# Scattering second choices between the experts' first tiles: a metaformer block with a top-2 mixture of experts on one core

## The chip, the cores and the metric

The kernel runs on one core of a Trainium2 chip. The metric is the device time of one execution in microseconds (us); lower is better. The engines are TensorE (PE), VectorE (DVE), ScalarE (ACT), GpSimd (POOL) and SyncE (SP), which here only issues DMAs and waits. "Line" and L followed by a number mean a line of the kernel before.

## What is computed

The input x is 128 images x 256 channels x 9 x 9 pixels, float32. A first part normalises each pixel over its channels, computes an attention-like convolution block and adds it to x. The second part, in which the change lies, is a mixture of experts over the 128 x 81 = 10368 tokens t (one token is one pixel of one image, 256 channels):

```
logits = layernorm(t) @ Wr.T + br                 # 8 experts
p      = softmax(logits); p1,e1,p2,e2 = top 2 of p
y      = p1 * ffn[e1](layernorm(t)) + p2 * ffn[e2](layernorm(t))
ffn[e](v) = gelu(v @ W1[e] + b1[e]) @ W2[e] + b2[e]   # 256 -> 512 -> 256
out    = t + y
```

Each token so goes to two experts, its first and its second choice; there are 20736 (token, expert) rows in all.

## The kernel before

**Stages.** Until about 733 us the first part runs, and leaves the tokens in SBUF. Then come three stages: routing (733 to 980 us), the experts' tiles (985 to 1510 us), and the sum of both results with the store of the output (to 1600 us).

**Routing** goes over the 81 pixels q in eight batches (6, six times 12, 3). Per batch PE turns the pixels (L637), ACT copies them out of PSUM (`turned`, L1382), DVE takes statistics (`pixel_parts`, L1045), computes probabilities and both choices (`choices`, L1087) and then the position of every row in its expert's region in DRAM (`positions`, L1115), with the help of two small PE products (`places`, L662). Position means: `base_s` (the expert's next free row) plus the number of earlier rows of that expert; first and second choices are counted together. ACT then builds one row block per pixel (`row`, L1407): 128 tokens x 260 numbers (256 channels, 4 tags) in `xf_s`, a ring of 18 slots. POOL scatters each block twice with an indirect DMA (L1546 to L1551), once to the first and once to the second choices' positions in `rows_d`: 162 scatters of 130 KB. A slot of the ring is taken again when both its scatters have landed (`landed`, L262; wait at L1413).

Beside this, SP loads the experts' weights in 32 pieces of 256 KB through three buffers (L378 to L381); ACT makes the high half (`high_piece`, L1418) and DVE the low half (`low_piece`, L1036) of each. Four pieces go with each batch; their places in the order of ACT and DVE are written out by hand (L1430 to L1448 and L1137 to L1146).

**Between routing and experts.** DVE gives the ends of the regions (`ends_c`, L1152), and SP writes 256 empty rows behind each expert's last row (L384 to L390). DVE computes the table `tabi_s` of 88 tiles (L1155 to L1180): for each tile of 256 rows its expert and its first row; then `base_c`. SP waits for the padding, all scatters, the table and the weights (L391 to L395), and starts the loads of rows. DVE waits for all scatters too, and then releases PE and ACT with `tab_r` (L1186).

**The experts' tiles.** There are always 88 tiles. For tile t: SP loads 256 rows (`load_rows`, L398), PE transposes them (`turn_rows`, L678), ACT and DVE split them into two float16 halves (L1454, L1188), PE multiplies (`up`, L689), ACT applies gelu, DVE splits again (L1218), PE multiplies (`down`, L707), DVE adds the bias (`scaled_rows`, L1225), ACT weighs the rows (`weighed`, L1470), POOL returns them with two indirect DMAs to `y_d` (`return_rows`, L1553). PE's order is transposes of t+1, up of t, down of t-1 (L728 to L733). ACT's order is `high_rows(t+1)`, `weighed(t-2)`, `gelu(t)` (L1482 to L1487). DVE ends an iteration with `scaled_rows(t-1)` and then `tags(t+1)`, which copies the tags out of the loaded rows and so frees their buffer. SP's turn t waits for the transposes and the tags of tile t and then loads tile t+2 into the same of two buffers:

```
with sp.Fori(1, TILES // 2 - 1) as i:
    for par in range(2):
        t = i * 2 + par
        sp.wait_ge(S["tt_p"], t + 1)
        sp.sem_inc(S["settle_s"], 1)
        sp.wait_ge(S["tag_c"], t + 1 + CREDIT)
        load_rows(t + 2, par)
```

`scaled_rows(t)` waits until the returns of tile t-2 have landed (L1228), as `yo_s` has two buffers.

## Time and profile before

| | us |
|---|---|
| median of 3 runs (lowest, highest) | 1610.61 (1609.75, 1611.9) |
| the profiled execution's own time | 1601.33 |
| its span, first to last instruction | 1599.6 |
| PE busy, share of the span | 1297.4, 81% |
| DVE busy | 1080.9, 68% |
| ACT busy | 771.0, 48% |
| POOL busy | 568.3, 36% |
| 162 scatters on POOL, L1549 | 158.6 busy |
| 176 returns on POOL, L1558 | 173.5 busy |

The profile comes from one execution, which took 9.3 us less than the median of the runs. Its page gives busy times over the whole span, so an engine with a small share can still be the last one in a stage. Other views give the same trace by stretches of time, by line of the kernel, or as the chain of work that ended last.

### The profile page before, as it was taken

The page shows a single profiled execution, that of the slowest core. Times are in us where ns is not written, and L with a number is a line of the kernel's source. Part 1 is how long each engine was busy: PE and PEld are TensorE (multiplying, and loading weights), DVE is VectorE, ACT ScalarE, POOL GpSimd, SP SyncE. Part 2 cuts the span into 40 slices and gives each one's busy share as a digit, 9 for nine tenths or more (in the row PEclk, how much of TensorE's full clock was granted, in tenths as well). Part 3 has the DMA queues.
Part 4 walks back from the last instruction along what each step waited for, and adds up shares of the span by engine and source line. Part 5 has one row for each costly group of instructions (what it writes and reads, how often), then busy time and mean ns, then how long its engine had stood idle before and what let it go on. Part 6 is the DMA issues. An engine that isn't in the chain of part 4 may idle for free.

```text
span 1599.6 us, 36879 instructions
## 1 busy us (share of the span) xinstructions
PE 1297.4 (81%) x9796; PEld 1072.9 (67%) x9797; DVE 1080.9 (68%) x2553; ACT 771.0 (48%) x1828; POOL 568.3 (36%) x561
## 2 busy tenths in 40 slices
PE   0197999999999999977656403999999999999592
PEld 0196999857676666657556302888888888888441
DVE  6797555378878788884656662777777777777462
ACT  0295666455444544442677761544555555555200
POOL 0163111333444334430577773333333333333200
PEclk9998999999999999985555555999999999999897
DMA  8635783858877978741243453222222222222297
GB/s 325 143 89 225 304 320 135 246 140 187 190 183 179 209 175 192 178 105 47 82 151 130 150 192 114 89 83 87 92 93 93 85 90 93 89 87 77 99 424 310
DMA packets 256214, 251.16 MB, mean 157 GB/s; under 512 B 149753, under 2 KB 234190, under 8 KB 251876
## 3 DMA queue, kind: packets, MB, share of 16 engines
q1 hardware_dynamic: 235789, 197.20, 41.1%
q0 software_dynamic: 20320, 53.45, 9.7%
q8 instruction: 18, 0.29, 0.1%
q14 instruction: 21, 0.17, 0.0%
q10 hardware_dynamic: 66, 0.05, 0.0%
HBM read 152.34 MB, written 105.75 MB: 161 GB/s over the span
## 4 chain that ended last, share of the span: by engine, by line
PE 56%; DVE 16%; DMA 10%; issue 6%; ACT 4%; SPq 3%; POOL 2%; DVEq 1%; ACTq 0%; POOLq 0%
PE ps L716 15%; PE ps L701 14%; PE ps L520 5%; PE ps L500 4%; PE ps L539 3%; DMA u_d<-in_zstrings 3%; PE ps L685 2%; DMA pool_<-k_d 2%; DMA pool_<-y_d 2%; POOL rows_d L1549 2%; PE ps L566 2%; SPq L291 2%; DMA pool_<-in_ffn_w 2%; PE ps L489 2%; ACT aux L1414 2%
## 5 line engine op out<-in xcount | busy, mean ns | idle before, releaser
L1558 POOL DMA_INDIRECT y_d<-pool_,to_s x176 | 173.5, 986 | 357.3 <-ACT pool_ L1473 328.0
L716 PE MATMUL ps<-pool_,aux 128*128 x2112 | 246.9, 273 | 4.9 <-DVE aux L1223 3.2
L701 PE MATMUL ps<-aux,pool_ 128*128 128x256 f16 x2112 | 247.1, 274 | 0.8 <-ACT aux L1466 0.6
L716 PEld LDWEIGHTS ps<-pool_,aux 128*128 128x128 f16 x2112 | 199.0, 98 | 47.4 <-issue 23.6
L701 PEld LDWEIGHTS ps<-aux,pool_ 128*128 x2112 | 207.2, 98 | 25.6 <-issue 1.4
L1549 POOL DMA_INDIRECT rows_d<-aux,idx_s x162 | 158.6, 979 | 105.7 <-ACT aux L1416 60.8
L1466 ACT ACTIVATE aux<-ps,b_s 128x256 f32<-128x256 f32 x352 | 138.1, 474 | 92.6 <-DVE aux L1223 92.5
L1458 ACT ACTIVATE aux<-ps 128x512 f16<-128x512 f32 x88 | 52.5, 597 | 187.0 <-PE ps L685 187.0
L1543 POOL DMA_DIRECT2D pool_<-v_d x64 | 50.0, 781 | 214.6 <-PE ps L599 213.2
L1231 DVE SCALAR_TENSOR_TENSOR pool_<-ps,pool_ 128x512 f32<-128x512 f32 x88 | 60.8, 691 | 92.4 <-PE ps L716 92.4
L539 PE MATMUL ps<-pool_,se_w_s 81*81 81x512 f32 x256 | 115.5, 593 | 3.6 <-DMA pool_<-k_d 3.6
L1223 DVE TENSOR_TENSOR aux<-aux 128x1024 f16<-128x1024 f32 x88 | 107.8, 1225 | 3.1
L1371 ACT ACTIVATE pool_<-ps,pool_ 128x81 f32<-128x81 f32 x256 | 79.5, 336 | 52.1 <-DVE pool_ L932 52.1
L883 DVE COPY aux<-ps 81x512 f32<-81x512 f32 x64 | 44.0, 687 | 71.5 <-PE ps L500 71.4
L685 PE MATMUL ps<-ident_s,pool_ 128*128 128x128 f32 x352 | 53.9, 276 | 44.1 <-DMA pool_<-rows_d 44.1
L520 PE MATMUL ps<-pool_,aux 82*128 82x162 f32 x512 | 85.6, 309 | 0.0
L1050 DVE BATCH_NORM_STATS2 aux<-big 128x6 f32<-128x256 f32 x81 | 45.0, 603 | 58.7 <-ACT big L1385 58.7
L665 PE MATMUL ps<-aux,before_s 128*128 128x8 f32 x16 | 4.8, 371 | 97.2 <-DVE aux L1112 97.2
L1473 ACT ACTIVATE pool_<-pool_,wrow_s 128x256 f32<-128x256 f32 x176 | 78.9, 498 | 9.1 <-DVE pool_ L1231 9.1
L1359 ACT ACTIVATE pool_<-ps,sa_ab 128x324 f32<-128x324 f32 x64 | 39.7, 620 | 86.6 <-PE ps L551 86.6
L1525 POOL COPY aux<-big 128x324 f32 x64 | 29.2, 457 | 138.6 <-PE ps L500 129.0
L1190 DVE TENSOR_TENSOR aux<-ps,aux 128x512 f16<-128x512 f32 x88 | 60.1, 683 | 24.8 <-ACT aux L1458 24.8
(204 smaller groups left out, 2974.4 us busy)
## 6 DMA issues: line engine op xcount, KB each, us to landing
pool_<-rows_d SPq DMA_DIRECT2D x88, 260.0 KB
pool_<-y_d SPq DMA_DIRECT2D x18, 1152.0 KB, 12.9
big<-in_x SPq DMA_DIRECT2D x2, 5184.0 KB, 21.2
xn_d<-big SPq DMA_DIRECT2D x8, 1296.0 KB, 4.8
v_d<-aux SPq DMA_DIRECT2D x64, 162.0 KB, 2.5
ks_d<-aux SPq DMA_DIRECT2D x64, 162.0 KB, 3.1
pool_<-xn_d SPq DMA_DIRECT2D x32, 324.0 KB
pool_<-k_d SPq DMA_DIRECT2D x32, 324.0 KB
```

The costliest lines, as they stand in the source:

```text
L500: last = nc.tensor.matmul(ps[0:HW, 4 + par, c * BS:(c + 1) * BS], xq_s[:, par, c, :], ident_s[:, :], start=True, stop=True)
L520: last = nc.tensor.matmul(o, pt_s[:, par, c, :], m_s[:, side, k * QUAD + c, :, :] .rearrange("p v n -> p (v n)"), start=True, stop=True)
L539: last = nc.tensor.matmul(ps[0:HW, n, :], se_w1_s[:, k, :], kq_s[:, par, k, 2 * n:2 * n + 2, :].rearrange("p b j -> p (b j)"), start=k == ...
L685: last = nc.tensor.transpose(ps[:, par, h * SLOTS + s * 128:h * SLOTS + (s + 1) * 128], rin_s[:, par, s, h * 128:(h + 1) * 128], ident_s[: ...
L701: last = nc.tensor.matmul(o, w_s[:, a, bass.ds(e * (4 * PIECE) + (k * HID + j * 128), 128)], xh_s[:, par, b, k * SLOTS:(k + 1) * SLOTS], s ...
L716: last = nc.tensor.matmul(ps[:, 6 + par, s * C:(s + 1) * C], hh_s[:, par, a, j, s * 128:(s + 1) * 128], w_s[:, b, bass.ds(e * (4 * PIECE) ...
L1223: nc.vector.tensor_tensor(lo, hf_s, hi, ALU.subtract).then_inc(S["hlo_c"], 1)
L1371: ins = nc.scalar.activation(e_s[:, par, h, b, :], ps[:, 2 + h, b * HW:(b + 1) * HW], ACT.Exp, bias=sm_s[:, par, 2, j:j + 1], accum_out=sm ...
L1466: nc.scalar.activation(hf_s[:, j * SLOTS:(j + 1) * SLOTS], ps[:, 2 + 2 * par + j // 2, (j % 2) * SLOTS:(j % 2 + 1) * SLOTS], ACT.Gelu, bia ...
L1473: ins = nc.scalar.activation(yo_s[:, par, s, :], yo_s[:, par, s, :], ACT.Copy, scale=wrow_s[:, par, s:s + 1])
L1549: nc.gpsimd.indirect_dma_start(out=rows_d[:, :], out_offset=bass.IndirectOffsetOnAxis(ap=idx_s[:, k, q:q + 1], axis=0), in_=xf_s[:, q % RI ...
L1558: nc.gpsimd.indirect_dma_start(out=y_d[:, :], out_offset=bass.IndirectOffsetOnAxis(ap=to_s[:, par, k:k + 1], axis=0), in_=yo_s[:, par, k, ...
```

## The change

First choices and second choices get separate counts, so that in each expert's region all first choices stand ahead of all second choices. During routing POOL scatters only first choices. SP stores the row blocks, three pixels at a time, plainly in a new DRAM tensor `xrow_d`. `SURE` = 33 is the number of tiles that hold only first choices whatever the routing (full tiles: at least (10368 - 8 x 255) / 256); the table of tiles now gives these full tiles of all experts first, then the rest, with 16 entries in place of 8. After the table DVE computes the second choices' positions (`idx2f_c`). SP loads the stored blocks back, three pixels (`THIRD`) at a time in 27 batches b, through two buffers `late_s`, and POOL scatters them in between the returns: 6 ahead of the first return, then 75 spread over 29 tiles (`late_before`). In SP's order a batch is loaded in turn `late_turn(b)`, behind the load of rows of that turn, after a wait for all scatters of batch b-2.

```diff
+THIRD = 3
+LATE = HW // THIRD
+SURE = -(-(BS * HW - EXPERTS * (SLOTS - 1)) // SLOTS)
+        xrow_d = dram("xrow_d", [HW, 128, WIDE])
+        def late_before(t):
+            return min(HW, 2 * THIRD + (HW - 2 * THIRD) * t // (SURE - 4))
+        def late_turn(b):
+            return 1 + min(t for t in range(SURE) if late_before(t) >= (b - 1) * THIRD)
...
-            for n in range(PIECES):
+            def load_piece(n):
                 if n >= 3:
                     sp.wait_ge(S["wlo_c"], n - 2)
                 sp.dma_start(stage_s[:, n % 3], ffn_w[n]).then_inc(S[f"wst_in{n % 3}"], 16)
+            def keep_rows(q):
+                sp.wait_ge(S["xft_c"], q + THIRD)
+                slot = q % RING
+                sp.dma_start(xrow_d[q:q + THIRD].rearrange("q b c -> b q c"),
+                             xf_s[:, slot:slot + THIRD, :]).then_inc(S[f"rst{slot // THIRD}"], 16)
+            for j in range(len(BATCHES)):
+                for n in range(4 * j, 4 * j + 3):
+                    load_piece(n)
+                for q in range(FIRST[j], FIRST[j + 1] - THIRD, THIRD):
+                    keep_rows(q)
+                load_piece(4 * j + 3)
+                keep_rows(FIRST[j + 1] - THIRD)
...
+            def load_late(b):
+                if b >= 2:
+                    sp.wait_ge(S[f"late_out{b % 2}"], b // 2 * (16 * THIRD))
+                sp.dma_start(late_s[:, b % 2], xrow_d[b * THIRD:(b + 1) * THIRD].rearrange("q b c -> b q c")
+                             ).then_inc(S[f"late_in{b % 2}"], 16)
+            def next_rows(t, par):
+                sp.wait_ge(S["tt_p"], t + 1)
+                sp.sem_inc(S["settle_s"], 1)
+                sp.wait_ge(S["tag_c"], t + 1 + CREDIT)
+                load_rows(t + 2, par)
             load_rows(0, 0)
             load_rows(1, 1)
+            sp.wait_ge(S["idx2f_c"], 1)
+            for b in range(2):
+                load_late(b)
+            for t in range(SURE - 2):
+                next_rows(t, t % 2)
+                for b in range(2, LATE):
+                    if late_turn(b) == t:
+                        load_late(b)
+            for k in range(2):
+                sp.wait_ge(S[f"late_out{k}"], 16 * THIRD * len(range(k, LATE, 2)))
+            for t in range(SURE - 2, SURE - 2 + SURE % 2):
+                next_rows(t, t % 2)
...
@@ choices, positions (DVE); places (PE) takes 16 columns
-                link(nc.vector.tensor_tensor(hot_s[:, 2, 0:n, :], hot_s[:, 0, 0:n, :], hot_s[:, 1, 0:n, :], ALU.add))
-                nc.vector.reduce_sum(tot_s[:, :], hot_s[:, 2, 0:n, :].rearrange("p s e -> p e s"),
+                nc.vector.reduce_sum(tot_s[:, :, :], hot_s[:, :, 0:n, :].rearrange("p k s e -> p k e s"),
-                    link(nc.vector.tensor_tensor(at_s[:, s + 1, :], at_s[:, s, :], hot_s[:, 2, s, :], ALU.add))
+                    link(nc.vector.tensor_tensor(at_s[:, s + 1], at_s[:, s], hot_s[:, :, s, :], ALU.add))
-                nc.vector.tensor_copy(idx_s[:, 1, lo:hi], top_s[:, 0, 0:n]).then_inc(S["idx_c"], 1)
...
@@ the table (DVE)
-            for e in range(1, EXPERTS):
+            for e in range(1, 2 * EXPERTS):
                 link(nc.vector.tensor_tensor(ends[:, e:e + 1], ends[:, e:e + 1], ends[:, e - 1:e], ALU.add))
-            full = [1, TILES, EXPERTS]
+            full = [1, TILES, 2 * EXPERTS]
...
+            link(nc.vector.tensor_copy(starts[:, full_ones], firsts[:, full_ones]))
+            link(nc.vector.tensor_tensor(starts[:, 1:EXPERTS], firsts[:, 1:EXPERTS], firsts[:, one_less], ALU.subtract))
+            link(nc.vector.tensor_tensor(spread_s, pos2_s[:, :].unsqueeze(2).to_broadcast(wide),
+                                         region_s[:, :].unsqueeze(1).to_broadcast(wide), ALU.is_ge))
+            link(nc.vector.tensor_tensor(spread_s, spread_s, starts[:, full_ones].unsqueeze(1).to_broadcast(wide), ALU.mult))
+            link(nc.vector.reduce_sum(moved, spread_s, axis=AX.X))
+            link(nc.vector.tensor_tensor(moved, moved, pos2_s[:, :], ALU.add))
+            nc.vector.tensor_copy(idx_s[:, 1, :], moved).then_inc(S["idx2f_c"], 1)
             for k in range(RING):
                 dve.wait_ge(S[f"scat{k}"], landed(HW - RING + (k - HW) % RING))
+            for g in range(RING // THIRD):
+                dve.wait_ge(S[f"rst{g}"], kept(g))
...
                     act.wait_ge(S[f"scat{slot}"], landed(q - RING))
+                    act.wait_ge(S[f"rst{slot // THIRD}"], 16 * (q // RING))
...
@@ POOL
-                for k in range(2):
-                    nc.gpsimd.indirect_dma_start(
-                        out=rows_d[:, :], out_offset=bass.IndirectOffsetOnAxis(ap=idx_s[:, k, q:q + 1], axis=0),
-                        in_=xf_s[:, q % RING, :], in_offset=None).then_inc(S[f"scat{q % RING}"], 16)
+                nc.gpsimd.indirect_dma_start(
+                    out=rows_d[:, :], out_offset=bass.IndirectOffsetOnAxis(ap=idx_s[:, 0, q:q + 1], axis=0),
+                    in_=xf_s[:, q % RING, :], in_offset=None).then_inc(S[f"scat{q % RING}"], 16)
...
-            with pool.Fori(0, TILES // 2) as i:
+            pool.wait_ge(S["idx2f_c"], 1)
+            sent = 0
+            for t in range(SURE - SURE % 2):
+                for q in range(sent, late_before(t)):
+                    b = q // THIRD
+                    pool.wait_ge(S[f"late_in{b % 2}"], 16 * (b // 2 + 1))
+                    nc.gpsimd.indirect_dma_start(
+                        out=rows_d[:, :], out_offset=bass.IndirectOffsetOnAxis(ap=idx_s[:, 1, q:q + 1], axis=0),
+                        in_=late_s[:, b % 2, q % THIRD, :], in_offset=None).then_inc(S[f"late_out{b % 2}"], 16)
+                sent = late_before(t)
+                return_rows(t, t % 2)
+            with pool.Fori(SURE // 2, TILES // 2) as i:
                 for par in range(2):
                     return_rows(i * 2 + par, par)
```

## Rows read from the trace of the kernel before

**Rows 1.** Busy time of each engine in two stretches: window, us, engines, PEclk, DMA share, GB/s

```profile
955.00:985.00 30.00, 0.00 (x0) 0.00 (x0) 7.55 (x25) 0.00 (x0) 19.33 (x20) 0.50 0.51 174
...
1005.00:1200.00 195.00, 194.26 (x1743) 168.82 (x1741) 141.92 (x336) 98.60 (x234) 65.38 (x67) 1.00 0.27 89
```

**Rows 2.** Chain that ended last, 980 to 990 us: start, us, what

```profile
979.16 2.43 DMA rows_d<-aux,idx_s
...
981.65 0.03 SPq L393
...
981.72 0.03 SPq L393
...
982.14 0.28 SPq L399
...
982.88 0.42 SPq L400
...
984.06 2.93 DMA pool_<-rows_d
...
987.03 1.11 PE ps L685 x4
```

**Rows 3.** Line L685, the transposes of a tile: duration ns, first and last start

```profile
L685 PE MATMUL ps<-ident_s,pool_ x352: 272/273/474, 985.5 to 1489.0; 128*128 128x128 f32 x176
```

**Rows 4.** Line L1549, the scatters: duration ns min/median/max, and landing

```profile
L1549 POOL DMA_INDIRECT rows_d<-aux,idx_s x162: 956/960/1365, 759.8 to 979.2; - x162
...
DMA to landing us min/median/max: 2.4/2.4/4.6
```

**Rows 5.** Chain that ended last, routing, around one load of weights

```profile
892.91 3.58 DMA pool_<-in_ffn_w
...
897.15 0.98 ACT big L1385
```

**Rows 6.** Timeline from 950 to 963 us: start, us, engine, line, operation

```profile
950.84 0.19 ACT L1416 ACTIVATE aux<-ptag_s 128x4 f32<-128x4 f32 x1
...
952.91 9.28 SPq L387 DMA_DIRECT2D rows_d<-aux  x8
...
956.74 1.39 DVE L1164 TENSOR_TENSOR til_s<-til_s 128x1 f32<-128x1 f32 x7
...
958.16 0.88 DVE L1168 TENSOR_TENSOR aux<-til_s,turn_s 1x704 f32<-1x704 f32 x1
...
963.08 0.19 DVE L1180 CAST tabi_s<-aux 1x88 int32<-1x88 f32 x1
```

**Rows 7.** Timeline of one tile in the steady stretch, all engines

```profile
1052.38 0.60 PE L685 MATMUL ps<-ident_s,pool_ 128*128 128x128 f32 x4
...
1053.32 0.16 DVE L1196 COPY tag_s<-pool_ 128x8 f32<-128x8 f32 x1
...
1053.60 0.90 ACT L1473 ACTIVATE pool_<-pool_,wrow_s 128x256 f32<-128x256 f32 x2
...
1054.30 12.18 SPq L400 DMA_DIRECT2D pool_<-rows_d  x3
...
1055.37 0.98 POOL L1558 DMA_INDIRECT y_d<-pool_,to_s  x1 [3.48 <-ACT pool_ L1473]
...
1056.66 0.98 POOL L1558 DMA_INDIRECT y_d<-pool_,to_s  x1 [0.30 <-issue]
```

**Rows 8.** Line L381, the issues of weight loads on SP's queue

```profile
L381 SPq DMA_DIRECT2D pool_<-in_ffn_w x32: 340/341/1079, 733.9 to 951.0; - x32
```

**Rows 9.** Chain that ended last, an early and a late tile's transposes

```profile
1000.25 0.44 PE ps L685 x4
...
1488.81 0.44 PE ps L685 x4
```

**Rows 10.** Lines L1221 and L1042 on VectorE: duration ns min/median/max

```profile
L1221 DVE CAST aux<-aux x88: 682/685/693, 994.2 to 1501.1; 128x1024 f16<-128x1024 f32 x88
...
L1042 DVE SCALAR_TENSOR_TENSOR pool_<-pool_ x32: 679/683/728, 776.7 to 954.9; 128x512 f16<-128x512 f32 x32
```

More of the change, by code:

```diff
@@ L1151, in _ @@
             nc.vector.tensor_copy(zero_s[:, :, C + 1:C + 2], pad_s[:, :].unsqueeze(2))
-            nc.vector.tensor_copy(tili_s[:, 1, :], base_s[:, :]).then_inc(S["ends_c"], 1)
+            firsts, starts, ends, weighted = (til_s[:, k, :] for k in range(4))
+            full_ones, rest = slice(0, EXPERTS), slice(EXPERTS, 2 * EXPERTS)
+            last_row = ends[:, full_ones]
+            link(nc.vector.tensor_tensor(firsts[:, full_ones], base_s[:, 0], region_s[0:128, :], ALU.subtract))
+            link(nc.vector.tensor_tensor(last_row, base_s[:, 1], firsts[:, full_ones], ALU.add))
@@ L1153, in _ @@
+            nc.vector.tensor_copy(tili_s[:, 1, :], last_row).then_inc(S["ends_c"], 1)
             for n in range(4 * len(BATCHES) - 3, PIECES):
                 low_piece(n)
[L1155 to L1160 removed]
@@ L1170, in _ @@
[L1170 to L1174 removed]
+            counts = weighted[:, full_ones]
@@ new lines, in _ @@
+            link(nc.vector.tensor_tensor(counts, last_row, region_s[0:128, :], ALU.subtract))
+            link(nc.vector.tensor_scalar(counts, counts, float(SLOTS - 1), None, ALU.add))
+            for value, tiles in ((firsts[:, full_ones], starts[:, full_ones]), (counts, starts[:, rest])):
+                link(nc.vector.tensor_copy(tili_s[:, 0, :], value))
+                link(nc.vector.tensor_scalar(tili_s[:, 0, :], tili_s[:, 0, :], SLOTS.bit_length() - 1, None,
+                                             ALU.arith_shift_right))
+                link(nc.vector.tensor_copy(tiles, tili_s[:, 0, :]))
@@ new lines, in _ @@
+            link(nc.vector.tensor_tensor(starts[:, rest], starts[:, rest], starts[:, full_ones], ALU.subtract))
+            link(nc.vector.tensor_copy(ends, starts))
+            for e in range(1, 2 * EXPERTS):
+                link(nc.vector.tensor_tensor(ends[:, e:e + 1], ends[:, e:e + 1], ends[:, e - 1:e], ALU.add))
+            link(nc.vector.tensor_scalar(weighted, starts, -1.0, None, ALU.mult))
+            behind = slice(EXPERTS - 1, 2 * EXPERTS - 1)
+            link(nc.vector.tensor_tensor(weighted[:, behind], weighted[:, behind], starts[:, full_ones], ALU.add))
@@ new lines, in _ @@
+            behind, one_less = slice(EXPERTS, 2 * EXPERTS - 1), slice(0, EXPERTS - 1)
+            link(nc.vector.tensor_tensor(weighted[:, behind], weighted[:, behind], starts[:, one_less], ALU.subtract))
+            full = [1, TILES, 2 * EXPERTS]
+            link(nc.vector.tensor_tensor(tcmp_s, ends[0:1, :].unsqueeze(1).to_broadcast(full),
+                                         turn_s[:, :].unsqueeze(2).to_broadcast(full), ALU.is_le))
+            link(nc.vector.reduce_sum(tab_s[:, 0, :], tcmp_s, axis=AX.X))
@@ L1175, in _ @@
+            link(nc.vector.tensor_tensor(tab_s[:, 0, :], tab_s[:, 0, :], tab_s[:, 3, :], ALU.add))
             link(nc.vector.tensor_tensor(tab_s[:, 1, :], tab_s[:, 1, :], tab_s[:, 2, :], ALU.mult))
```

77 lines of the change are left out of this document (36 added, 41 removed).

## The prediction, made before the changed kernel was run

> **What bounds the kernel now.** I read first the busy times by stage. From 1005 to 1200 us PE is busy 194.26 of 195 us at a granted clock of 1.00: the experts' tiles are PE's. From 955 to 985 us PE, ACT and nearly DVE stand still, and POOL works: the end of routing is POOL's [rows 1]. So the change can gain in a stretch that waits for POOL alone, and it puts new work beside a stretch in which PE has no slack.
>
> Second, the chain of waits at that seam. The last scatter starts at 979.16 and lands 2.43 us later; SP then runs through waits at some 0.065 us each and a load of a register, issues the first loads of rows at 982.88 and 984.06, and PE has turned to the second tile at 987.03 [rows 2]. The first tile's transposes start at 985.5 [rows 3], so a load of rows lands 2.6 us after its issue when alone. The scatters take 0.96 us each, with 0.30 us between (next row of POOL: 1.27 us in all); they land after 2.4 us, at worst 4.6 [rows 4].
>
> Third, whether POOL holds routing itself back. It does not: in the chain of that stage a load of weights (3.58 us), ACT's copies and DVE follow each other, each round through them [rows 5]; no wait of ACT for a slot of the ring is in it. POOL's 24 scatters of a batch take 30.4 us where the round takes about 29, so POOL only falls behind: the last row is built at 950.84 + 0.19 = 951.03 [rows 6], 28 us before the last scatter starts. That lag is what the change can remove, and not all of it, as SP's padding and DVE's table stand behind it.
>
> **What the change removes.** With one scatter per pixel POOL keeps pace, and the last one lands near 951 + 1.3 + 2.4 = 955 us. What is late next? SP's padding begins at 952.91, has eight issues over 9.28 us and one more behind, and lands near 965 (landing priced as a scatter's 2.4). The table: L1180 ends at 963.08 + 0.19 = 963.27 [rows 6]. It grows. Eight more dependent additions of some 0.20 us (1.39 / 7): 1.6. Four operations over 88 x 16 = 1408 numbers in place of 704: 704 numbers take 0.88, of which some 0.15 is the fixed part of the smallest operations, so +0.74 each, 2.95. Eight further small linked operations less some that fall away (a second shift to tiles, `weighted`, the fold of the expert's number): 1.85. Sum 6.4, table at 969.7. In routing DVE loses an addition and a cast per batch and gets a wider sum, which I take as nothing, hidden or within 0.1 us a batch. SP's `keep_rows` moves between loads of weights: most stores wait for rows that are there before the next piece's buffer is free. Only in the last batch of 12 does the store of the third group wait about 2 us longer than piece 27's buffer, and 400 KB go ahead of it. I take +0.7, between 0 and the 3.6 us of a slow load [rows 5] as the upper end. `base_c` at 970.4.
>
> Behind the table there is new work ahead of `tab_r`: seven operations for the second choices' positions, three of them over 648 numbers at about 0.82 each, 3.3 us with the rest, and then DVE's 26 waits one after another, 26 x 0.065 = 1.7 [rows 2]. PE is so released at 975.4 and turns to the second tile 1.5 us later (985.5 to 987.03), at 977.0. SP's path to the same point, 0.1 + 0.74 + 1.18 + 2.93 = 4.95 us behind the table, gives 975.4 and hides. **Gain: 987.03 - 977.0 = 10.0 us.**
>
> **What it adds in the tiles.** Turn t of SP loads tile t+2 and then, in 25 of its turns 1 to 28, waits for the scatters of a batch. Queued behind that wait is the load of tile t+3. Follow it from PE's transposes of tile t+1, which start at 1052.38 [rows 7]:
> - ACT weighs tile t-2 behind `high_rows(t+1)`; done at 1053.60 + 0.90, 2.12 us after the start.
> - POOL starts the returns of t-2 0.87 later, at 1055.37; both take 1.29 + 0.98 = 2.27. Now 5.26.
> - The scatters stand ahead of the next return, so behind this one. The one that completes the batch is the first, second or third (p); gap 0.30, (p-1) x 1.27, landing 2.4: 2.7, 4.0 or 5.2.
> - SP wakes, issues the batch's load (0.34 as for the loads of weights [rows 8], plus 0.1), passes three waits (0.2), loads its register (0.74): 1.4; the rows land 2.6 later.
>
> Sum 5.26 + 2.7 + 1.4 + 2.6 = 11.97 for p = 1, 13.2 and 14.5 for p = 2 and 3. What needs them is the transposes of tile t+3, two tiles on. A tile takes (1488.81 - 1000.25) / 84 = 5.82 us [rows 9], two 11.64. So the links cost 0.3, 1.6 and 2.9 us. Without the wait SP issues that load at tags + 0.82 (1053.32 + 0.16 to 1054.30), which leaves it some 1.4 us of slack: enough for none of the dearer two. The stall delays PE, through that ACT and POOL, and the next link starts from there: it repeats. By `late_before` p is 1, 2, 3 in 9, 10, 5 of the 24 batches behind the first, mean 1.83, mean excess 1.4. Links span two tiles: 14 x 1.4 = 19.5. At the end SP waits once more for the last scatter before it loads tile 33, p = 3 without an issue between: 2.4. Together 22; laid out tile by tile, with the turns that have no batch, I get 21. **Loss: 21 us**, tiles of 6.5 in place of 5.82 through the first 32.
>
> POOL too is full there. A tile has 2.27 + 0.30 for the returns and 2.59 x 1.28 for scatters, 5.9 against 5.82: 1.5 us over 29 tiles if it were the only bound, nothing beside tiles of 6.5. Before, it was busy 65.38 of 195 us [rows 1]. Traffic grows: 75 blocks of 133 KB read and written are 20 MB over some 190 us, about 105 GB/s on top of 89 [rows 1]; the engines' share goes from 0.27 to perhaps 0.6. The landings, not shown under this mix, are bounded by 2.4 and 4.6 [rows 4]; I take 2.4, the median beside a busy POOL. At 3.1 for every landing the same walk gives 31 us in place of 21.
>
> DVE's cast L1221 takes 0.685 us for 1024 numbers, twice the pace of L1042's 0.683 for 512 [rows 10]. Before, returns never lay beside it; now scatters will. L1042 ran beside POOL's scatters in routing and varied by 0.05 only, so I price the meeting at 0, and at most the cast's 0.69 once a link: 12.5 x 0.69 = 8.6 us. The Trainium skill (SBUF — State Buffer, "Who interferes with whom") says that a cast in a mode that uses both of VectorE's port pairs shuts GpSimd out for its whole length, descriptors included. By that rule the loss would be near the 8.6 us; no row here shows it.
>
> **Sum.** -10 + 21 = +11 us. Against the profiled execution's own 1601.3 that is 1612.3; it was 9.3 us under the median, and I carry the difference over: 1610.6 + 11 = 1621.6.
>
> **Rivals.**
> *The waits hold nothing back* (0.20). SP's wait ends before the next load is due: all landings and issues together would have to be 1.3 us shorter than priced for p = 2. For it: slack of 1.4 us per load, and 2.4 is the median of landings. Against: the sums above lack a reserve; p = 3 would need 2.8. Then only POOL's 1.5 remains: -10 + 1.5, 1602.
> *DVE's cast holds POOL, or landings stretch* (0.15). Against it, L1042's even times and the free DMA engines. It decides once the cast starts while a scatter is being written. +11 + 8.6, or +21 by landings: 1630 to 1632.
> *The seam does not shorten* (0.10): loads of weights wait behind stores of rows in every batch, up to 1.5 us in seven, so the tail's 10 us are spent in routing. For it, the loads are links of the chain [rows 5]; against it, half of the scatters' traffic goes. +21, 1632.
> The forecast has 0.50, the rest (0.05) is spread.
>
> **How the numbers follow.** A measurement of this kernel can tell about 0.2%, 3.2 us. The forecast's own range is +4 to +18 us, 1614.6 to 1628.6. Slower gets nearly all of the forecast and the two dear rivals, 0.70; faster most of the first rival, 0.18; 0.12 lies between, mainly where waits of SP cost half of what I say. The range from 1603 to 1637 takes in part of the first rival and the dear ones with their bounds.
>
> **What would show it.** Right: PE's second transposes near 977; a period of tiles 3 to 32 near 6.5 us that returns to 5.82 behind tile 33; in the waits, L685 on the load of rows for about 20 us in all, in steps of 0.3 to 3; SP's loads of rows issued 1 us after the late loads and not after the tags; POOL busy over 80% there. Wrong: even tiles of 5.82 with loads of rows on time (first rival); scatters of over 1.1 us beside L1221, or casts longer than 0.69 (second); the last block built after 955 us (third). The time is wrong, with the mechanism right, if landings under the new traffic are not near 2.4 us.

## The result, and the profile of the changed kernel

| | before | changed |
|---|---|---|
| median of the runs (lowest, highest), us | 1611.26 (1609.75, 1614.53), 4 runs | 1643.88 (1641.5, 1645.34), 4 runs |
| profiled execution, own time and span, us | 1601.33, 1599.6 | 1645.34, 1643.6 |
| ratio to before, 95% interval | | 1.0198 (1.0178 to 1.0218) |

The changed kernel is 32.6 us slower. Of all runs in this document one, of e10 (1631.81 us), was in the slow state of the chip, and it is left out of the medians and ratios. The forecast was +11 us, 1621.6, with a range that ended at 1637. The direction was right, the size was not. In this part L and a number mean a line of the kernel that a fence or sentence is about; in the changed kernel L734 is the transposes of a tile (before L685), L750 and L765 the two products, L1296 the cast and L1298 the subtraction of the hidden values (before L1221 and L1223), L1624 the scatters of first choices, L1643 the late scatters, L1633 the returns, L432 and L439 SP's loads of rows and of a late batch.

The page of the changed kernel, busy time by engine and three groups of instructions (line, operation, tensors, count, then busy us and mean ns, then the idle time ahead):

```profile
PE 1315.4 (80%) x9796; PEld 1074.4 (65%) x9797; DVE 1086.1 (66%) x2563; ACT 773.5 (47%) x1828; POOL 575.7 (35%) x561
...
L1633 POOL DMA_INDIRECT y_d<-pool_,to_s x176 | 174.1, 989 | 285.2 <-ACT pool_ L1549 196.6
...
L1624 POOL DMA_INDIRECT rows_d<-aux,idx_s x81 | 79.2, 977 | 161.9 <-ACT aux L1492 145.1
...
L1643 POOL DMA_INDIRECT rows_d<-aux,idx_s x81 | 87.2, 1077 | 49.1 <-issue 25.6
```

Over the whole span next to nothing has changed, as the shares are averages. The same window by stage, against [rows 1], shows the loss: PE has gone from 194.3 busy us in 195 to 166.9, and POOL from 65 to 126.

```profile
core 0: us, PE busy (x) PEld busy (x) DVE busy (x) ACT busy (x) POOL busy (x), PEclk, DMA share, GB/s
1000.00:1195.00 195.00, 166.85 (x1372) 134.29 (x1370) 108.55 (x265) 80.21 (x185) 125.80 (x122) 0.96 0.53 163
```

Where the time went, from the starts of a tile's transposes in both traces (tile 3 means the fourth):

| stretch | before | changed | difference |
|---|---|---|---|
| start to the first row block built (both kernels run the same code) | 759.3 | 763.6 | +4.3 |
| from there to the second tile's transposes | 227.7 | 217.6 | -10.1 |
| second tile to tile 3 | 13.1 | 13.5 | +0.4 |
| tile 3 to tile 34 (31 tiles) | 180.6 | 227.6 | +47.0 |
| tile 34 to tile 87 | 308.0 | 310.3 | +2.3 |
| from there to the end | 110.9 | 111.1 | +0.2 |

The seam gave what it was to give, and the loss is in the tiles with late scatters, 7.34 us a tile in place of 5.83. The first line is no part of the change. The same stage took 759.3 to 772.8 us in the eleven profiles of this study, and the profile of before is the shortest of them; the median of the runs stands nearer +32.6 than the +44 of the two profiles for that reason at least in part. What else lies between the two numbers stays open.

The seam in the changed kernel, from the timeline (start, us, engine, line, operation):

```profile
963.27 2.87 DVE L1219 TENSOR_TENSOR til_s<-til_s 128x1 f32<-128x1 f32 x15
...
966.79 1.61 DVE L1228 TENSOR_TENSOR aux<-til_s,turn_s 1x1408 f32<-1x1408 f32 x1
...
975.15 0.20 DVE L1242 CAST tabi_s<-aux 1x88 int32<-1x88 f32 x1
...
978.53 0.20 DVE L1253 CAST idx_s<-aux 128x81 uint32<-128x81 f32 x1
...
979.82 1.12 PE L734 MATMUL ps<-ident_s,pool_ 128*128 128x128 f32 x4 [34.04 <-DVEq L1261]
```

The four operations over 1408 numbers take 1.61 us each where 0.88 plus 0.74 was priced. From the last low half (961.31) the table takes 14.04 us where it took 7.68: +6.36, priced 6.4. From the table to PE it is 4.5 us, priced 5.0.

The waits of SP and of PE between 1000 and 1220 us (who waited, for what: us in total, times, longest):

```profile
SPq L439 <- DMA rows_d<-aux,idx_s: 133.0, 22, 8.4
SPq L431 <- DVE tag_s L1271: 21.3, 6, 6.4
SPq L444 <- DMA rows_d<-aux,idx_s: 8.6, 1, 8.6
```

```profile
PE ps L734 <- DMA pool_<-rows_d: 18.4, 15, 3.2
PE ps L750 <- issue: 11.1, 20, 0.8
```

SP stands at the wait ahead of a late load nearly all of the time, and the load of the next tile's rows behind it. PE waits 15 times for rows, 18.4 us, which is close to the "about 20 us in all" of the prediction. But that is not the whole price. Ahead of the next products PE stands another 0.8 us at most, 11.1 us in 20 times, for which the view names no releaser, and at times its clock is lower behind a wait. One link with all its parts, in the chain that ended last (start, us, what):

```profile
1028.35 0.65 PE ps L734 x4
...
1036.54 2.69 DMA rows_d<-aux,idx_s
...
1039.24 0.38 SPq L439
...
1039.75 0.39 SPq L431
...
1040.57 4.08 DMA pool_<-rows_d
...
1044.77 1.11 PE ps L734 x4
```

This is a link with p = 3, from tile 8 to tile 10. The prediction's terms up to the third scatter's start, 5.26 and 2.8, give 1036.41, and the trace 1036.54. The landing takes 2.69 (priced 2.4), SP's path 1.34 (priced 1.4), the rows 4.08 + 0.13 (priced 2.6). So 16.4 us in place of 14.5, and the rows' landing is 1.6 of the 1.9. Behind the wait of 3.15 us that this left to PE, the granted clock was at its lower level, 1.2 GHz, for 6.8 us:

```profile
1044.20:1051.00 6.80, 6.12 (x28) 4.32 (x29) 1.75 (x7) 2.23 (x5) 3.15 (x4) 0.50 0.48 127
1051.00:1060.00 9.00, 9.00 (x84) 7.97 (x83) 4.23 (x11) 3.79 (x9) 4.54 (x5) 1.00 0.33 116
```

The columns are those of the window above; 0.50 and 1.00 are the granted clock. There were four such stretches between tiles 3 and 34, 17 us together (at 1044.2, 1068.1, 1105.6 and 1214.8), and none in that part of the trace of before. Counted on PE's side, the 47 us between tiles 3 and 34 are 31 us more of idle time (31.6 against 0.6) and 16 us more of busy time (196.0 against 179.9). About 8 of these 16 are PE's work in the four stretches at half clock; the others lie mainly in instructions ahead of a pause, which the trace shows longer, and were not followed up.

### The profile page after: what moved, and what is told of

Read it like the earlier page. It is cut to its first block, busy times and chain, and to the rows that moved or that the text cites. A ratio compares the mean times of both kernels' runs of the same rounds, so it can differ in the third digit from the quotient of the medians.

```text
span 1643.6 us, 36813 instructions
## 1 busy us (share of the span) xinstructions
PE 1315.4 (80%) x9796; PEld 1074.4 (65%) x9797; DVE 1086.1 (66%) x2563; ACT 773.5 (47%) x1828; POOL 575.7 (35%) x561
## 4 chain that ended last, share of the span: by engine, by line
PE 52%; DVE 15%; DMA 15%; issue 7%; ACT 5%; SPq 4%; POOL 0%; DVEq 0%; ACTq 0%; POOLq 0%
PE ps L750 12%; PE ps L765 12%; PE ps L568 5%; PE ps L548 3%; DMA pool_<-rows_d 3%; DMA u_d<-in_zstrings 3%; PE ps L734 2%; DMA rows_d<-aux,idx_s 2%; PE ps L587 2%; PE ps L795 2%; ACT aux L1490 2%; DMA pool_<-k_d 2%; PE ps L614 2%; SPq L307 2%; DMA pool_<-in_ffn_w 2%
## 5 line engine op out<-in xcount | busy, mean ns | idle before, releaser
L1633 POOL DMA_INDIRECT y_d<-pool_,to_s x176 | 174.1, 989 | 285.2 <-ACT pool_ L1549 196.6
L750 PE MATMUL ps<-aux,pool_ 128*128 128x256 f16 x2112 | 253.2, 278 | 12.2 <-issue 11.1
L765 PE MATMUL ps<-pool_,aux 128*128 x2112 | 247.0, 273 | 7.6 <-DVE aux L1298 3.3
L750 PEld LDWEIGHTS ps<-aux,pool_ 128*128 x2112 | 207.5, 100 | 46.1 <-issue 18.9
L765 PEld LDWEIGHTS ps<-pool_,aux 128*128 128x128 f16 x2112 | 199.3, 98 | 51.3 <-issue 27.2
L1306 DVE SCALAR_TENSOR_TENSOR pool_<-ps,pool_ 128x512 f32<-128x512 f32 x88 | 60.8, 691 | 139.2 <-PE ps L765 139.2
L1624 POOL DMA_INDIRECT rows_d<-aux,idx_s x81 | 79.2, 977 | 161.9 <-ACT aux L1492 145.1
L1298 DVE TENSOR_TENSOR aux<-aux 128x1024 f16<-128x1024 f32 x88 | 107.8, 1225 | 3.1
L1643 POOL DMA_INDIRECT rows_d<-aux,idx_s x81 | 87.2, 1077 | 49.1 <-issue 25.6
L734 PE MATMUL ps<-ident_s,pool_ 128*128 128x128 f32 x352 | 56.1, 284 | 53.3 <-DVEq L1261 34.0
L1549 ACT ACTIVATE pool_<-pool_,wrow_s 128x256 f32<-128x256 f32 x176 | 78.9, 498 | 9.3 <-DVE pool_ L1306 9.3
L714 PE MATMUL ps<-aux,before_s 128*128 128x16 f32 x16 | 4.9, 384 | 96.7 <-DVE aux L1160 96.7
L734 PEld LDWEIGHTS ps<-ident_s,pool_ 128*128 128x128 f32 x352 | 41.4, 145 | 60.2 <-DVEq L1261 34.1
```

The costliest lines, as they stand in the source:

```text
L734: last = nc.tensor.transpose(ps[:, par, h * SLOTS + s * 128:h * SLOTS + (s + 1) * 128], rin_s[:, par, s, h * 128:(h + 1) * 128], ident_s[: ...
L750: last = nc.tensor.matmul(o, w_s[:, a, bass.ds(e * (4 * PIECE) + (k * HID + j * 128), 128)], xh_s[:, par, b, k * SLOTS:(k + 1) * SLOTS], s ...
L765: last = nc.tensor.matmul(ps[:, 6 + par, s * C:(s + 1) * C], hh_s[:, par, a, j, s * 128:(s + 1) * 128], w_s[:, b, bass.ds(e * (4 * PIECE) ...
L1298: nc.vector.tensor_tensor(lo, hf_s, hi, ALU.subtract).then_inc(S["hlo_c"], 1)
L1549: ins = nc.scalar.activation(yo_s[:, par, s, :], yo_s[:, par, s, :], ACT.Copy, scale=wrow_s[:, par, s:s + 1])
L1624: nc.gpsimd.indirect_dma_start(out=rows_d[:, :], out_offset=bass.IndirectOffsetOnAxis(ap=idx_s[:, 0, q:q + 1], axis=0), in_=xf_s[:, q % RI ...
```

## The experiments

All times stand beside runs of the kernel before on the same chip.

| kernel | median, us | before, us | ratio (95%) | us a tile, tiles 3 to 34 |
|---|---|---|---|---|
| changed | 1643.88 | 1611.26 | 1.0198 (1.0178 to 1.0218) | 7.34 |
| e1_four_buffers | 1627.88 | 1609.95 | 1.0111 (1.0076 to 1.0146) | 6.59 |
| e2_small_loads | 1646.32 | 1609.95 | 1.0233 (1.0187 to 1.0279) | 7.00 |
| e3_stores_behind | 1645.55 | 1609.95 | 1.0226 (1.0187 to 1.0264) | 7.31 |
| e4_one_turn_later | 1624.23 | 1609.95 | 1.0088 (1.0060 to 1.0116) | 6.66 |
| e5_one_input | 1609.81 | 1609.55 | 1.0017 (0.9979 to 1.0055) | 6.26 |
| e6_straight | 1606.94 | 1609.55 | 0.9969 (0.9935 to 1.0002) | 6.01 |
| e7_split_positions | 1612.40 | 1611.38 | 0.9998 (0.9981 to 1.0015) | 6.06 |
| e8_after_one_input | 1648.23 | 1611.38 | 1.0246 (1.0212 to 1.0279) | 7.26 |
| e10_two_in_front | 1606.9 | 1612.96 | 0.9967 (0.9947 to 0.9988) | 6.09 |

The last column is from one profile each.

### Four buffers: does SP's wait make the loss?

`BUFS` is 4.

```diff
-        late_s = take_aux(128, 2, THIRD, WIDE)
+        late_s = take_aux(128, BUFS, THIRD, WIDE)
...
-                if b >= 2:
-                    sp.wait_ge(S[f"late_out{b % 2}"], b // 2 * (16 * THIRD))
+                if b >= BUFS:
+                    sp.wait_ge(S[f"late_out{b % BUFS}"], b // BUFS * (16 * THIRD))
```

> Four buffers for the late batches in place of two, nothing else. SP then waits for the scatters of batch b-4, which are long done, and no load of rows stands behind such a wait. Theory W (the wait of SP for the last scatters holds the loads of rows back, tile by tile): tiles 3 to 33 fall from a mean of 7.3 us to 5.9 to 6.2, what is left being POOL's own work (2.3 for the returns, 2.6 scatters of 1.3 to 1.4 us); the time falls by 35 to 50 us, to 1594 to 1609, under the kernel before. PE's halved clock in that stretch goes too, as it follows from PE's idle gaps. Rival P (POOL is the bound, with scatters stretched by VectorE's cast and subtraction): POOL's sum of about 6.2 us a tile stays, and so does a loss of some 10 us; but if P alone explained the 7.3 us, the time would stay near 1644. Rival T (the traffic stretches the loads): bytes are the same, so the time stays within 10 us of 1644.

Measured: 1627.88 us, ratio 1.0111 where the changed kernel has 1.0198, so 14 us less (16 by the medians). Waits of SP and PE, 1000 to 1220 us:

```profile
SPq L432 <- DVE tag_s L1272: 151.0, 32, 8.8
SPq L444 <- DMA rows_d<-aux,idx_s: 12.3, 1, 12.3
```

```profile
PE ps L766 <- DVE aux L1299: 9.9, 8, 2.3
PE ps L735 <- DMA pool_<-rows_d: 6.8, 1, 6.8
```

SP now waits only for the tags, as before the change, and once at the handoff for the last late scatters; there PE waits 6.8 us for one tile's rows. Of the 47 us in the tiles 23 are gone, so SP's wait was the cause of about half. The expectation, 35 to 50 us less with tiles of 5.9 to 6.2, was missed: the tiles still take 6.59, not 5.83. Of the 24 us that are left, 10 lie in the two steps at the handoff (tile 32 to 33 takes 12.93 us and 33 to 34 takes 8.93, before 5.76 and 5.96), the rest in the tiles ahead of it. POOL's rows in the same kernel, 1000 to 1195 us (count, busy us, mean ns, idle ahead):

```profile
L1644 POOL DMA_INDIRECT rows_d<-aux,idx_s x75 | 83.1, 1108 | 22.9 <-issue 22.9
L1634 POOL DMA_INDIRECT y_d<-pool_,to_s x60 | 65.8, 1096 | 24.2 <-issue 23.9 <-ACT pool_ L1550 0.3
```

POOL works back to back. With 0.30 between, a tile costs it 2.59 x (1.108 + 0.30) + 2 x (1.096 + 0.30) = 6.4 us, where the prediction had 5.9: both kinds of its DMA instructions have become longer. Why is in the timeline:

```profile
1063.75 0.69 DVE L1297 CAST aux<-aux 128x1024 f16<-128x1024 f32 x1
...
1064.47 1.23 DVE L1299 TENSOR_TENSOR aux<-aux 128x1024 f16<-128x1024 f32 x1
...
1064.87 1.67 POOL L1644 DMA_INDIRECT rows_d<-aux,idx_s  x1 [0.30 <-issue]
...
1066.84 0.96 POOL L1644 DMA_INDIRECT rows_d<-aux,idx_s  x1 [0.31 <-issue]
```

The scatter of 1.67 us began while the subtraction L1299 ran, which reads two tensors in SBUF; the next one, beside neither, takes 0.96. Sorted over the whole stretch of e1: 42 scatters beside neither, mean 0.961; 22 beside the subtraction alone, mean 1.385, longest 1.67. The 11 others lay beside the cast, two of them beside it alone (0.96) and nine beside cast and subtraction (mean 1.15, longest 1.44).

The cast lengthens scatters too. The changed kernel has the clearest place:

```profile
1060.43 0.69 DVE L1296 CAST aux<-aux 128x1024 f16<-128x1024 f32 x1
1060.53 1.41 POOL L1643 DMA_INDIRECT rows_d<-aux,idx_s  x1 [0.30 <-issue]
...
1061.15 1.23 DVE L1298 TENSOR_TENSOR aux<-aux 128x1024 f16<-128x1024 f32 x1
```

This scatter began 0.10 us behind the cast and ended 0.82 us after the cast's end, as the one of 1.67 us ended 0.83 us after the subtraction's end. Between tiles 3 and 34 of the changed kernel 22 of POOL's 137 indirect DMAs were lengthened, by 8.5 us in all: eight by the subtraction (5.4 us) and 14 by the cast (3.1 us). All but two of them ended 0.82 to 0.84 us after the end of the operation that was running when they began; the two ended 0.12 us after the end of a cast that began beside them. In e1 it is 12.6 us by the subtraction and 4.1 by the cast. The 13 scatters of the changed kernel beside the cast alone took 0.96, but there the cast came late in the scatter and gave way itself, up to 0.81 us in place of 0.685.

### One late load of 16-byte pieces: what does the transfer cost?

```diff
+                from_ = 0 if b < 2 else C
-                sp.dma_start(late_s[:, b % 2], xrow_d[b * THIRD:(b + 1) * THIRD].rearrange("q b c -> b q c")
+                sp.dma_start(late_s[:, b % 2, :, from_:WIDE],
+                             xrow_d[b * THIRD:(b + 1) * THIRD, :, from_:WIDE].rearrange("q b c -> b q c")
```

> Late batches 2 to 26 load only the four tag columns of their rows (16 bytes of 1040); the channels in the scattered second-choice rows are those of earlier batches, so that part of the computation is left out. Waits, scatters and their order are as in the changed kernel; the 390 KB that stand in the queue ahead of each load of rows become 6 KB (in as many pieces). Theory W with the transfer as a term of it: rows land 2.6 to 3.0 us after their issue in place of 3.0 to 4.1; 0.8 us less on each link of two tiles, 10 to 14 us in all and up to 8 more if the clock no longer halves: 1622 to 1634. Rival T (traffic is nearly all of the loss): 1595 to 1610. If the transfer is no term, the time stays at 1644.

The profile agrees with a transfer that costs about 10 us: tiles of 7.00 in place of 7.34 (-10.4 us over 31), and the rows that the chain waits for land in 2.84 us on the mean of 14 (1.89 to 3.33) where the changed kernel has 3.60 (2.98 to 4.08). SP's wait stays (134.2 us in 23 times). But the median is no shorter, 1646.32 where 1622 to 1634 was expected, and the profiled execution was the shortest of five that spread over 15 us, so the time does not confirm it. The number of descriptors is also the same. Inconclusive for the size; it does rule out that the bytes of the late loads alone make the loss.

### Stores behind the weight loads

```diff
-                for q in range(FIRST[j], FIRST[j + 1] - THIRD, THIRD):
-                    keep_rows(q)
                 load_piece(4 * j + 3)
-                keep_rows(FIRST[j + 1] - THIRD)
+                if j < len(BATCHES) - 2:
+                    for q in range(FIRST[j], FIRST[j + 1], THIRD):
+                        keep_rows(q)
+            for q in range(FIRST[len(BATCHES) - 2], HW, THIRD):
+                keep_rows(q)
```

> Only the order of SP in routing differs: the stores of the rows go behind all four loads of weights of their batch, and those of the last two batches behind the last piece of weights. Theory S (the stores, and SP's waits for rows ahead of piece 4j+3, delay the last pieces of weights, and these the table): the last low half ends at 956 to 957 us in place of 961.3, the table at 970 to 971 in place of 975.3, and the time falls by 4 to 5 us, to about 1639. Rival: the pieces are late from the stores' traffic itself, wherever it stands in the queue: less than 2 us.

From the first to the last row block it is 190.2 us, against 193.1 in the changed kernel and 191.5 before; the first tile's transposes come 213.4 us after the first row block, in place of 216.2. So the stores did hold the weights back by 2 to 3 us, between the 4 to 5 us of theory S and the under 2 us of its rival. The time, 1645.55, shows nothing of it: its interval of +-0.4% is wider than the effect.

### The late load one turn later

```diff
         def late_turn(b):
-            return 1 + min(t for t in range(SURE) if late_before(t) >= (b - 1) * THIRD)
+            return 2 + min(t for t in range(SURE) if late_before(t) >= (b - 1) * THIRD)
```

> Each late batch is loaded one turn of SP later, still with two buffers. SP then comes to the wait about 5.8 us later, when the scatters of batch b-2 have landed; POOL gets each batch later and may wait for it instead. Theory W: SP's waits for scatters shrink from 133 us to under 20, the loads of rows are on time again; POOL waits some 1 us a batch for its rows, which PE does not see until POOL's lag reaches the returns: 1600 to 1620. Rivals P and T: no change, 1640 to 1648.

1624.23 us with two buffers only, as good as four. SP still waits for scatters, 93.1 us in 23 times in place of 133.0, but the longest wait is 5.6 us and not 8.4, and the load of rows behind it is early enough again. The expectation had the direction right and the sizes too good: under 20 us of SP's waits, and 1600 to 1620 us. It was not the number of waits that cost, nor the buffers, but that the wait was asked before its scatters could be done. Both kernels end at the same bound, POOL (6.59 and 6.66 us a tile): in e4 too it works back to back, with 3.6 of 195 us idle beyond the gaps between its instructions.

### The subtraction with one input

```diff
-                nc.vector.tensor_tensor(lo, hf_s, hi, ALU.subtract).then_inc(S["hlo_c"], 1)
+                nc.vector.tensor_scalar(lo, hf_s, 0.0, None, ALU.mult).then_inc(S["hlo_c"], 1)
```

This edit was made in e5 to the version with four buffers, and in e8 to the changed kernel alone. It leaves out the low halves of the hidden values.

> Four buffers as in the run before, and VectorE's subtraction of the high from the full hidden values (two inputs in SBUF, 1.23 us) is replaced by a product of one input with 0, so the low halves of the hidden values are left out. In the four-buffer run POOL worked back to back, its scatters and returns taking 0.96 to 1.00 us alone or beside the cast, and 1.2 to 1.7 us beside the subtraction. Theory L (an operation of VectorE with two SBUF inputs holds POOL up): all of POOL's indirect DMAs take 0.96 to 1.05 us now; POOL's sum falls from 6.4 to 5.9 us a tile; tiles 3 to 33 take 6.0 to 6.2 us in place of 6.6; the time falls by 10 to 18 us. Rival K (it is the cast, an operation in a fast mode with one input, and the new product too, in the same mode): the stretched DMAs stay or get more, and the tiles stay at 6.4 or more.

> The changed kernel itself, two buffers and SP's wait included, with VectorE's two-input subtraction replaced by a one-input product with 0 (low halves of the hidden values left out). It prices the stretch of POOL's indirect DMAs where SP's wait rules. If scatters beside the subtraction lie on the links (scatter, landing, late load, load of rows, transposes), each link of two tiles shortens by 0.2 to 0.7 us: tiles 3 to 33 fall from 7.3 to 6.9 to 7.1 us, 8 to 14 us in all. If SP's wait alone sets the links, with scatters mostly away from the subtraction, less than 5 us.

POOL's rows of e5, in the same window as those of e1:

```profile
L1644 POOL DMA_INDIRECT rows_d<-aux,idx_s x75 | 77.5, 1033 | 22.9 <-issue 22.9
L1634 POOL DMA_INDIRECT y_d<-pool_,to_s x62 | 63.8, 1028 | 30.0 <-issue 30.0
```

Its timeline, the place that the long scatter had in e1, and one more:

```profile
1066.27 0.88 DVE L1297 CAST aux<-aux 128x1024 f16<-128x1024 f32 x1
...
1066.93 1.07 POOL L1644 DMA_INDIRECT rows_d<-aux,idx_s  x1 [0.30 <-issue]
1067.18 0.69 DVE L1299 TENSOR_SCALAR aux<-aux 128x1024 f16<-128x1024 f32 x1
```

```profile
1048.06 0.68 DVE L1297 CAST aux<-aux 128x1024 f16<-128x1024 f32 x1
1048.10 1.50 POOL L1644 DMA_INDIRECT rows_d<-aux,idx_s  x1 [0.30 <-issue]
...
1048.77 0.69 DVE L1299 TENSOR_SCALAR aux<-aux 128x1024 f16<-128x1024 f32 x1
```

Theory L expected all of POOL's indirect DMAs at 0.96 to 1.05 us, from the reading that the cast leaves them alone. They are not: the second place has 1.50 us behind the cast, where no subtraction of two SBUF inputs runs, and the seven scatters beside the product alone took 1.02 to 1.13. In the first place the cast itself took 0.88. So the edit did not take the cause away; what it put in place of the subtraction is over 0.53 us sooner, and POOL is held for less. That two inputs in SBUF are needed to hold POOL is refuted; what the number of inputs adds beyond the length is not shown.

Tiles go from 6.59 to 6.26, 10.2 us over 31, and the time from 1627.88 to 1609.81. The shorter replacement (0.69 against 1.23) also serves PE, which had waited 9.9 us for the subtraction in e1; the two effects of the edit are not told apart in the time, only in POOL's means. In the changed kernel the same edit changes next to nothing: 1648.23, tiles of 7.26, 2.4 us less over 31, as the expectation had it for a pace that SP's wait alone sets. That is the price list of the loss: with POOL partly relieved and SP's wait kept, 7.26 - 5.83 is 44 us over 31 tiles; with the wait relieved and POOL as it is, 6.59 - 5.83 is 24 us. They do not add, as the later of the two sets the pace.

### Towards a version that wins

The next three keep the idea, with all reasons found so far: four buffers, the late load issued one turn ahead of the turn that needs it, and fewer late scatters. The last 12 pixels' row blocks are still in the ring when routing ends, so their second choices are scattered straight from it and are neither stored nor loaded.

```diff
+STRAIGHT = 12
-LATE = HW // THIRD
+LATE = (HW - STRAIGHT) // THIRD
...
+            for q in range(HW - STRAIGHT, HW):
+                nc.gpsimd.indirect_dma_start(
+                    out=rows_d[:, :], out_offset=bass.IndirectOffsetOnAxis(ap=idx_s[:, 1, q:q + 1], axis=0),
+                    in_=xf_s[:, q % RING, :], in_offset=None).then_inc(S["ring_out"], 16)
```

**e6** computes the second choices' positions ahead of the table, so that these 12 can run beside it.

> Four buffers, and POOL's load in the tiles is cut: the positions of second choices are computed ahead of the table, the last 12 pixels' second choices are scattered straight from the ring while POOL would stand idle before the tiles (12 x 1.27 = 15 us from about 956), 12 more ahead of the first return, and the other 57 over 28 tiles, 2.04 a tile. Each late batch is loaded one turn before it is needed, when its buffer has been free for tiles. The last five stores of rows but one fall away. Theory W + L (the loss was SP's wait plus POOL's sum): POOL's sum is 2.2 + 2.2 + 1.2 = 5.7 us, under the 5.82 of PE; tiles 3 to 33 take 5.85 to 5.95 us; PE turns to the second tile 9 to 12 us earlier than before, measured from the first row; the time is 1598 to 1604, faster than both kernels by 0.4 to 0.7% of before. Rival T (traffic beside the loads of rows still holds tiles back): tiles of 6.1 or more, 1608 or more.

1606.94 us, ratio 0.9969, its interval just reaching 1, and above the expected 1598 to 1604; tiles of 6.01 where 5.85 to 5.95 was expected. The step at the handoff is gone. In its profile tile 34 begins 419.0 us after the first row block; before 421.4, changed kernel 458.7.

**e7** computes ahead of the table only the 12 pixels' positions, and the other 69 behind `tab_r`. `moved_on` holds the operations that the changed kernel has at L1247 to L1253, for some of the pixels; its first call stands ahead of the table.

```diff
+            moved_on(HW - STRAIGHT, HW)
...
             dve.sem_inc(S["tab_r"], 1)
+            moved_on(0, HW - STRAIGHT)
```

> The version before it with one thing moved: ahead of the table only the 12 pixels that are scattered straight from the ring get their second positions (three operations of 96 numbers in place of 648, 0.25 us in place of 0.84 each); the other 69 follow behind the release of PE, while the first rows are on their way, and the late loads wait for them. From the traces so far: the table comes 1.8 to 2.5 us earlier, PE's first transposes 2 us earlier, measured from the first row; tiles as before, 5.9 to 6.05 us. Time 1.5 to 2.5 us under the version before it, 0.994 to 0.996 of the kernel before. If the late loads, which now start some 4 us later, hold the scatters ahead of the first return back, POOL loses at most that, with 20 us of idle time before the first return: no change from it.

1612.40, no gain where 1.5 to 2.5 us were expected. PE's first transposes come 1.4 us earlier than in e6, measured from the first row block. That was lost at once, in the chain at tile 2:

```profile
986.62 0.38 SPq L445
...
987.04 0.49 SPq L445
...
989.44 6.08 DMA pool_<-rows_d
...
995.65 0.79 PE ps L741 x4
```

The first four late loads (1.56 MB) are issued in one go, and the rows of tile 2 stand behind them: they land in 6.08 us, and PE turns to tile 2 11.9 us after it began the first transposes (983.8).

**e10** puts only two of them in front.

```diff
-AHEAD = BUFS * THIRD
+FRONT = 2
+AHEAD = FRONT * THIRD
-            for b in range(BUFS):
+            for b in range(FRONT):
                 load_late(b)
```

> The version before it in this study with two of its four first late loads (0.78 MB) in front of the load of tile 2's rows, and the other two behind the loads of tiles 2 and 3; 6 scatters ahead of the first return and 63 over 28 tiles (2.25 a tile) in place of 12 and 57. Nothing of the computation is left out. Theory Q (the 6.1 us landing of tile 2's rows is the queue of late loads ahead of it): tile 2's transposes start some 9 us behind the second tile's in place of 11.9, its rows land in 4 to 4.5 us, and the kernel gains 2 to 3 us: 1608 to 1610 on a chip where the kernel before takes 1611, ratio 0.998 to 0.999; the denser scatters may give back up to 1 us of it, tiles of 6.05 to 6.1 us. Rival (the rows of tile 2 land late because of the scatters' traffic and of the positions, not of the queue): tile 2 at 11 us or more behind, ratio 0.9998 as before or above. If the time rather goes to 0.995 or below, early scatters of POOL had also delayed the first returns.

The distance is 8.5 us in place of 11.9, as the queue's theory has it, and the rows of tile 2, issued at 991.30, have landed by 994.93. The ratio is 0.9967 (0.9947 to 0.9988), some 5 us under the kernel before; against e7's 0.9998 that is about 5 us, more than the 2 to 3 us that the theory gave, but short of the 0.995 at which the expectation would have named another cause. Where the surplus comes from stays open. e10 and e6 are alike within their intervals, and e10 is the one that beats both kernels beyond its interval. Its tiles take 6.09 us, and POOL's late scatters now 1.205 us on the mean (23 beside the subtraction alone took 1.56):

```profile
L1662 POOL DMA_INDIRECT rows_d<-aux,idx_s x64 | 77.1, 1205 | 19.6 <-issue 19.6
L1648 POOL DMA_INDIRECT y_d<-pool_,to_s x64 | 66.0, 1031 | 34.2 <-issue 26.8 <-ACT pool_ L1564 7.4
```

## Why the prediction was right in direction and wrong in size

- **The seam, -10.0 us: right.** Measured -10.1 against the first row block. The table (+6.36 for 6.4) and the way to PE (4.5 for 5.0) hold; the stores cost 1.6 us between the first and the last row block where 0.7 was taken, less than the upper end of 3.6.
- **The mechanism in the tiles: right.** SP's wait ahead of the late load holds the load of the next tile's rows (e1 removes it, e4 moves it, and both halve the loss in the tiles). The rival "the waits hold nothing back" is refuted by the 18.4 us in which PE waited for rows and by e1.
- **"Sum 5.26 + 2.7 + 1.4 + 2.6", the loss of 21 us: the step that failed.** Measured 47. POOL's terms and SP's 1.4 hold to a tenth in the link shown. The last term, the rows' landing at 2.6, doesn't: 3.60 on the mean of the 14 links in the chain; the scatters' took 2.52 where I took 2.4. That is 1.1 us a link. Counted over 14 links it is 16 us; by the prediction's own walk, which has 31 us for landings of 3.1 each, 6.2 together where 6.12 was measured, it is 10. I had priced the scatters' landing beside a busy POOL and then took the rows' landing from a place with no other traffic, though in this very change a load of 390 KB stands right in front of them; the sentence "At 3.1 for every landing the same walk gives 31 us in place of 21" named the danger and stopped short of it. That it is the load right in front, and not the traffic as such, fits e1: by the times at which the rows' semaphores were raised, the loads of rows issued between 1005 and 1195 us landed in 2.67 us on the mean before, 3.67 in the changed kernel and 2.96 in e1, which moves the same late batches but has no load of rows right behind one.
- **What the walk left out.** It let PE go on at full pace as soon as the rows are there. The trace has four stretches of half clock, 17 us, which cost about half their length, some 8 us, and 11.1 us in which PE stood ahead of the next products. With the measured landings and the clock the sum is 39 to 45 of the 47 us; how much of the 11.1 lies on the chain, and what the rest is, stays open. This sum is arithmetic on the changed kernel's profile; e2 tested its largest term, which its profile bears out (10.4 us) and its time does not. That PE's pauses bring the lower clock is read from the order in the trace and was not tested.
- **"POOL too is full there ... nothing beside tiles of 6.5": half right.** In the changed kernel POOL was not the bound (e8). But its own sum is 6.4 us a tile and not 5.9, so that a cure for SP's wait alone stops at half of the way (e1, e4). I had not asked what comes next when the forecast's bound is removed.
- **The rival about DVE: its mechanism is there, its price was not.** Its sign of being wrong came true: scatters of over 1.1 us beside the cast (1.41 at 1060.53) and casts longer than 0.69 (up to 0.81). But in the changed kernel the cast lengthened POOL's instructions by 3.1 us in all, not by 0.69 once a link, and the subtraction behind it, which the prediction did not name, by 5.4. The row of the scatters [rows 4] had the sign of it: their durations read 956/960/1365, and I used the median. Four took over 1.3 us, all beside operations L1042 that read two tensors; this is one:

```profile
932.98 1.88 DVE L1042 SCALAR_TENSOR_TENSOR pool_<-pool_ 128x512 f16<-128x512 f32 x3
...
933.73 1.36 POOL L1549 DMA_INDIRECT rows_d<-aux,idx_s  x1 [0.30 <-issue]
```

I looked at whether L1042 was stretched (it was not, 0.05 us) instead of whether the scatter was.
- **The rival about the seam: wrong**, as the first point shows; it foresaw the right victim (weights behind stores), at 2 to 3 us in all.

By the Trainium skill (SBUF — State Buffer, "Who interferes with whom") a cast that uses both of VectorE's port pairs and GpSimd shut each other out, and the one that issues first goes first. The trace agrees: the scatter at 1060.53 ended only 0.82 us after the cast that was there first, and casts that met an indirect DMA under way took up to 0.98 us in e5 in place of 0.685. The same section says that an operation of VectorE with two inputs in SBUF contends with a GpSimd instruction that reads SBUF, and infers that this leaves the generation of descriptors alone: the first half agrees with the scatters of 1.67 us beside the subtraction, the inference does not.

## What to carry to other kernels

When a transfer is put on a queue ahead of another, price the second one's landing behind the first, not alone, and place a wait on that queue so late that its condition is already met: one turn later was worth as much here as twice the buffers. When an engine that used to idle becomes nearly full, read the maximum of its instructions' durations and find what lay beside the longest ones; compare ends with ends, as sorting by mere overlap hid the cast here. Then ask what its own sum is with that neighbour present in every round. Work that is taken off the end of one stage has to fit into the slack of the next: here it paid, by 0.3%, only when a seventh of it was no longer stored and loaded again.

## What the runs showed of the hardware that was not expected

- A scatter or return that GpSimd issues takes 0.96 to 1.0 us alone. When VectorE's subtraction of two SBUF tensors (1.23 us), its cast of 1024 numbers (0.685) or its one-input product (0.69) began 0.04 us or more before it and still runs, it ends 0.82 to 0.88 us after that operation, and so takes up to 1.67 us (1.71 for a return, in e1) behind the subtraction, 1.50 behind the cast and 1.13 behind the product alone. It kept 0.96 beside L1306, one of whose inputs lies in PSUM. A cast that meets it under way is itself longer, up to 0.98. With the subtraction replaced by the product the scatters' mean fell from 1.108 to 1.033.
- A load of a tile's rows landed in 2.6 us alone, in 2.98 to 4.08 behind one late load of 390 KB (2.84 on the mean when that load had as many pieces of 16 bytes), and in 6.08 behind four.
- The granted clock fell to half for 3.4 or 6.8 us at a time in the tiles of the changed kernel, after waits of PE. Stretches of that kind in the part ahead of routing, whose code no kernel here changes, were 6.8 us together in the shortest profile of that part and 23.9 in the longest (e6), and go broadly with the spread of its length of 759 to 773 us. This was read from the traces and not tested.
